# A second feed-forward pass moved from its own phase into the main steps

## The chip, the cores and the metric

The kernel runs on one core of a Trainium2 chip. TensorE multiplies, VectorE and ScalarE work on SBUF and PSUM, GpSimd works on SBUF, and SyncE issues most DMAs. The metric is the device time of one execution in microseconds; runs are compared by their median.

## The reference, cut to what matters

The input x is 32 images of 96 channels by 28 x 28 (784 tokens), float32. Three stages are each added to what they read:

```python
x = x + conv(_gn(x), ...)       # group norm, 4 experts of 96 -> 96 -> 96 by 1x1 convolutions, top 2 gated
t = tokens(x)
t = t + attn(_ln_t(t), ...)     # 12 heads of 8; fk = fv = where(t >= 0, t + 1, exp(t)); A = fk.v * gauss
t = t + ffn(_ln_t(t), W1, b1, W2, b2)
# ffn: y1 = x Wb1 + b1 (384 wide, weights are signs); h = gelu(quant(y1)); y2 = h Wb2 + b2; out = quant(y2)
# quant, per group of 6 images (5 groups; images 30 and 31 stay 0):
#   clip(a * 128 / (max|a| + 1e-5), -128 + 1e-5, 128 - 1e-5)
```

The quantisation needs the largest absolute value over six whole images before any of them can go on, once for y1 (384 channels) and once for y2 (96 channels).

## The kernel before, in words

A **setup** (to about 66 us) loads x, takes group-norm statistics, prepares weights and gates. Then there are two phases.

The **main phase** handles one image a step, as a software pipeline over three images: step i runs the experts of image i, the attention of image a = i - 1 and the first feed-forward pass of image f = i - 2. Steps 0 to 3 and 30 to 32 are written out, the others are a hardware loop over pairs. TensorE in a step: the expert hidden tiles (`hidden`, L994), transposes of the attended image to tokens (`to_tokens`, L862), x1 transposed to channels into slot 0, the expert mix (`mix`, L1010), keys and values in two parts (`kv`, L1055), transposes of tok2 into slot 2 and of t1cm into slot 1, the A matmuls (L1158), three up-projection tiles (`ffn_tile`, L1017 and L1020) with three small matmuls chained between them, and the output matmuls (L1187). PSUM is four slots of two banks; each slot has several users in a step, and each user waits for the reader before it.

ScalarE in a step (`step`, L748): three relus, copies from PSUM (tok2, xh1T, tok1, St, R), two exps (L759), the cast of the normalised tokens to `big`, and last `norm_image` (L725), which normalises image i + 2 and makes its f16 high part. VectorE (`step`, L1464): layer-norm statistics and apply (L1423, L1430, L1436), the residual t1cm, feature maps (L1470), the low part (L1514), the mask of A, the absolute maximum of each y1 tile straight from PSUM (`absmax`, L1440), t2T. GpSimd (`step`, L606): the low part of the next image (`xn_rest`, L578), and the inverse root of the variance for two layer norms (`rstd`, L598). Of the first feed-forward pass only the maxima of y1 are kept; the normalised tokens stay in `big` as two f16 parts, and SyncE stores t2 to `out` in HBM.

The **feed-forward phase** begins when all 30 maxima are there. For each image TensorE computes y1 once more (`ffn_up`, L1200), ScalarE applies gelu with the scale and casts the high part of two tiles (`gelu_tile`, `gelu_hi`, L813 and L819), VectorE makes the low parts and clips (`split`, L1550), TensorE projects down (`ffn_down`, L1210), ScalarE evacuates y2 (L829), VectorE takes its maximum, and after six images a scale; images of the group before are scaled, clipped and added to the stored t2, which SyncE loads back and stores (`clipped`, L1577). The last group of six follows alone.

All order is that of the five instruction streams as written; engines meet only at semaphores. A queue that waits holds all that is behind it.

## Time and profile before

| | us |
|---|---|
| median of 3 runs | 830.09 (829.99 to 832.92) |
| the profiled execution: span from first to last instruction | 829.6 |
| lowest timed run less that span (what lies around it) | 0.4 |
| PE busy, of the span | 769.0 (93%) |
| DVE busy | 636.5 (77%) |
| ACT busy | 476.7 (57%) |
| POOL busy | 180.2 (22%) |

The profiled execution has no time of its own beside its span in the profile, so the timed runs stand for it. Busy time is what an engine spent in instructions, averaged over stages with different limits; which wait ends last in a stage is read from that stage. PE is TensorE, DVE VectorE, ACT ScalarE, POOL GpSimd. L12 is line 12 of the kernel.

### The profile page before, as it was taken

Reading aid. Unit: us, or ns where it says so; the run is one execution under the profiler, and the core shown is the slowest. Engines: PE = TensorE matmul, PEld = TensorE weight load, DVE = VectorE, ACT = ScalarE, POOL = GpSimd, SP = SyncE. Lnnn points to the kernel's source line nnn. Section 1 sums busy time; section 2 is a strip of 40 time slices with the busy share of each in tenths; the row PEclk is TensorE's granted clock in tenths of the full one; section 3 lists DMA queues with packets and bytes.
Section 4 is the critical chain, followed back from the end, with each engine's and each line's share of the span. In section 5 each row is a group of like instructions: output and inputs, shape, how many; then the busy total and the mean of one; then the engine's idle time right before and its main releaser. Section 6 shows DMA issues by size and latency. Waiting matters only on the chain.

```text
span 829.6 us, 15136 instructions
## 1 busy us (share of the span) xinstructions
PE 769.0 (93%) x4663; PEld 510.4 (62%) x4663; DVE 636.5 (77%) x1945; ACT 476.7 (57%) x684; POOL 180.2 (22%) x209
## 2 busy tenths in 40 slices
PE   6798899999999999999999999999999999999991
PEld 3465566667666667666666766666766555555540
DVE  3576377877888878788877778887778468999997
ACT  2554445545555554545554555554553499988981
POOL 1440222332223232223232223233222000000000
PEclk8899989999999999999999999999999999999996
DMA  9950011101101101111110101010100101463333
GB/s 217 207 138 16 16 30 30 46 29 29 44 29 29 44 29 29 44 29 29 42 31 29 43 30 29 29 43 29 30 28 15 32 28 53 147 179 113 119 117 116
DMA packets 20351, 48.62 MB, mean 59 GB/s; under 512 B 4937, under 2 KB 5223, under 8 KB 20327
## 3 DMA queue, kind: packets, MB, share of 16 engines
q1 hardware_dynamic: 19928, 47.72, 21.0%
q10 hardware_dynamic: 399, 0.60, 0.3%
q8 instruction: 13, 0.21, 0.1%
q14 instruction: 11, 0.09, 0.0%
HBM read 29.51 MB, written 18.67 MB: 58 GB/s over the span
## 4 chain that ended last, share of the span: by engine, by line
PE 68%; DVE 11%; ACT 8%; issue 7%; SPq 3%; POOL 2%; DMA 1%; ACTq 0%; DVEq 0%; POOLq 0%
PE slot L1010 15%; PE slot L994 9%; PE slot L1017 7%; PE slot L1020 6%; PE slot L1158 6%; PE slot L1055 5%; PE slot L1187 5%; PE slot L1218 4%; PE slot L1222 4%; PE slot L862 4%; DVE stage L1470 4%; ACT stage L759 3%; SPq L442 3%; ACT hT L752 2%; PE slot L926 1%
## 5 line engine op out<-in xcount | busy, mean ns | idle before, releaser
L1436 DVE TENSOR_SCALAR tok<-tok,ln_mv,ln_rs 112x96 f32<-112x96 f32 x434 | 109.2, 322 | 58.2 <-POOL ln_rs L603 58.2
L1010 PE MATMUL slot<-hT,w2s 128*96 128x392 f32 x384 | 135.5, 503 | 3.0 <-ACT hT L752 2.3
L759 ACT ACTIVATE stage<-slot,minus_one 112x768 f32<-112x768 f32 x64 | 52.6, 822 | 125.6 <-PE slot L1055 123.3
L752 ACT ACTIVATE hT<-slot,b1c,w_unit 128x784 f32<-128x784 f32 x96 | 93.1, 1006 | 23.0 <-PE slot L994 23.0
L1010 PEld LDWEIGHTS slot<-hT,w2s 128*96 128x96 f32 x384 | 60.6, 164 | 64.1 <-issue 54.4
L603 POOL TENSOR_TENSOR ln_rs<-ln_ve,pow_half 112x7 f32<-112x7 f32 x62 | 91.8, 1481 | 4.8
L1017 PE MATMUL slot<-big,W1b 99*128 (+1 forms) x360 | 90.3, 332 | 2.1 <-ACT hT L816 0.6
L1020 PE MATMUL slot<-big,W1b 96*128 (+1 forms) x360 | 89.8, 330 | 0.0
L816 ACT ACTIVATE hT<-slot,s 128x784 f32<-128x784 f32 x90 | 80.3, 926 | 6.6 <-DVE stage L1554 6.3
L1442 DVE TENSOR_REDUCE ymax<-slot 128x784 f32 (+1 forms) x90 | 81.1, 956 | 0.1
L600 POOL TENSOR_TENSOR ln_ve<-ln_mv,ln_eps 112x7 f32<-112x7 f32 x62 | 12.5, 202 | 316.2 <-DVE ln_mv L1430 316.2
L1055 PEld LDWEIGHTS slot<-qkvw,xh1T 97*112 97x112 f32 x448 | 73.6, 177 | 10.5 <-issue 9.5
L1423 DVE BATCH_NORM_STATS2 ln_st<-tok 112x6 f32<-112x96 f32 x434 | 75.0, 243 | 4.7 <-ACT tok L746 2.6
L1055 PE MATMUL slot<-qkvw,xh1T 97*112 97x192 f32 x448 | 78.3, 326 | 0.1
L580 POOL TENSOR_TENSOR xn_lo<-xn,xn_hi 96x784 f16<-96x784 f32 x32 | 54.4, 1699 | 102.5 <-DVE tok L1436 102.5
L1470 DVE SCALAR_TENSOR_TENSOR stage<-stage,slot 112x768 f32<-112x768 f32 x64 | 51.8, 849 | 28.2 <-ACT stage L759 28.2
L1554 DVE SCALAR_TENSOR_TENSOR stage<-hT,stage 128x784 f16<-128x784 f32 x60 | 56.6, 968 | 14.5 <-ACT stage L825 14.5
L1158 PE MATMUL slot<-stage 112*96 112x96 f32 x448 | 46.8, 257 | 12.9 <-DVE stage L1470 12.9
L746 ACT COPY tok<-slot 112x672 f32<-112x672 f32 x62 | 44.5, 718 | 24.7 <-PE slot L862 24.7
L862 PE MATMUL slot<-con,tok 112*96 112x112 f32 x434 | 52.1, 260 | 2.2 <-DVE tok L1436 2.2
L1158 PEld LDWEIGHTS slot<-stage 112*96 112x96 f32 x448 | 41.5, 168 | 19.7 <-DVE stage L1470 19.7
L1218 PE MATMUL slot<-stage,W2b 128*96 128x392 f16 x240 | 46.6, 334 | 5.7 <-DVE stage L1554 2.0
(190 smaller groups left out, 1285.2 us busy)
## 6 DMA issues: line engine op xcount, KB each, us to landing
out<-t2T SPq DMA_DIRECT2D x56, 294.0 KB, 2.6
xs<-in_x SPq DMA_DIRECT2D x32, 294.0 KB, 2.8
big<-in_x SPq DMA_DIRECT2D x7, 1176.0 KB, 15.3
xs<-out SPq DMA_DIRECT2D x24, 294.0 KB, 3.3
...
```

The costliest lines, as they stand in the source:

```text
L603: nc.gpsimd.tensor_tensor(ln_rs[n][:, :], ln_ve[n][:, :], pow_half[0:TOK, 0:CHUNKS], ALU.pow).then_inc(ln_rstd[n], 1)
L752: nc.scalar.activation(hT[:, t, :].rearrange("p (a n) -> p a n", a=2), halves(t, P), ACT.Relu, scale=w1_unit[:, t:t + 1], bias=b1c[:, t:t ...
L816: nc.scalar.activation(gel[:, t, :].rearrange("p (a n) -> p a n", a=2), halves(t, P), ACT.Gelu, scale=s1[:, bass.ds(g, 1)]).then_inc(gelu_ ...
L862: return mm(o, i, ident[0:rows, 0:rows], start=start, stop=True, is_transpose=True, skip_group_check=True)
L1010: ins = mm(S[k][0:C, h, 0:HALF], w2s[:, v, t, :], hT[:, t, h * HALF:(h + 1) * HALF], start=t == 0, stop=t == TILES - 1, skip_group_check=True)
L1017: mm(S[k][:, h, 0:HALF], w, big[:, f, 0, h * HALF:(h + 1) * HALF], start=True, stop=False, skip_group_check=True)
L1020: ins = mm(S[k][:, h, 0:HALF], w[0:C, :], big[0:C, f, 1, h * HALF:(h + 1) * HALF], start=False, stop=True, skip_group_check=True)
L1055: ins = mm(chunks(k, n, 256, 2 * C)[:, j, :], xh1T[:, (j0 + j) * TOK:(j0 + j + 1) * TOK], qkvw[:, C:3 * C], start=True, stop=True, skip_gr ...
L1158: ins = mm(S[3][0:C, 0, 0:C], fkv[:, j, 0:C], fkv[:, j, C:2 * C], start=j == 0, stop=j == CHUNKS - 1)
L1436: ins = V.tensor_scalar(dst[:, j, :], src[:, j, :], ln_mv[n][:, j, 0:1], ln_rs[n][:, j:j + 1], ALU.subtract, ALU.mult)
L1442: V.tensor_reduce(ymax[:, bass.ds(3 * f + t, 1)], halves(k, P), AX.XY, ALU.max, apply_absolute_value=True).then_inc(ymax_done, 1)
L1470: V.scalar_tensor_tensor(fkv[:, j0:j0 + n, :], ekv[:, j0:j0 + n, :], 1.0, chunks(k, n, 256, 2 * C), ALU.min, ALU.max).then_inc(f_ready, 1)
```

## The change

There are now 40 written-out steps for every engine and no feed-forward phase. Step i also runs the gelu and split of image d = i - 9 and the down-projection of image e = i - 10, and finishes an image of the group before (i - 17 up to image 17, two a step in steps 35 to 37). The y1 tiles are kept in SBUF for eight images (ScalarE copies them out of PSUM, `keep_y1`), so the up-projection is done once; y2 is kept for eight images too. Maxima of y1 are taken from SBUF in the next step. Scales are made for one group at a time, in steps 8, 14, 20, 26, 32 for y1 and 16, 22, 28, 34 for y2, the last behind the steps. The cast of gelu's high part moves from ScalarE to GpSimd; scale, clip and add of most images move from VectorE to GpSimd in three operations. ScalarE normalises image i + 1 in the middle of step i instead of image i + 2 at its end. The transposes of t1cm go to slot 2 instead of slot 1, behind the reader of the tok2 transposes. The tiles share `over`, `big` and `stage` in another layout; the `two_ones` DMA is replaced by a memset. The last six images are finished by VectorE as before.

```diff
+Y1_RING, Y2_RING = 8, 8
+TO_GELU, TO_DOWN, TO_OUT = 9, 10, 17
+RB_IMAGES = 18
+STEPS = QIMAGES + TO_DOWN
+S1_STEP = {QB * g + QB + 2: g for g in range(QGROUPS)}
+S2_STEP = {QB * g + QB + TO_DOWN: g for g in range(QGROUPS)}
+OUT_STEP = {n + TO_OUT: [(n, "pool")] for n in range(RB_IMAGES)}
+OUT_STEP.update({35 + k: [(RB_IMAGES + 2 * k, "pool"), (RB_IMAGES + 2 * k + 1, "dve")] for k in range(3)})
+OUT_ORDER = [one for i in sorted(OUT_STEP) for one in OUT_STEP[i]]
+OUT_COUNT = {n: (by, sum(1 for m, b in OUT_ORDER if b == by and m <= n)) for n, by in OUT_ORDER}
...
+        x2 = sb("x2", [C + PARTS, 2, HW], F16)
+
+        def y1(b):
+            o = (Y2_RING + b % Y1_RING * TILES) * HW
+            return big[:, o:o + TILES * HW].rearrange("p (t n) -> p t n", n=HW)
+
+        def y2(b):
+            o = b % Y2_RING * HW
+            return big[0:C, o:o + HW]
...
+            def hi_part(d, t):
+                pool.wait_ge(gelu_ready, TILES * d + t + 1)
+                wait_count(pool, y2_ready, d - 1)
+                nc.gpsimd.tensor_copy(h_hi(d, t), y1(d)[:, t, :]).then_inc(hi_parts, 1)
+
+            outs = [0]
+
+            def finish(n):
+                pool.wait_ge(s2_ready, n // QB + 1)
+                nc.gpsimd.tensor_scalar(y2(n), y2(n), s2[:, n // QB:n // QB + 1], 1.0, ALU.mult,
+                                        ALU.mult).then_inc(y2_scaled, 1)
+                outs[0] += 1
+                pool.wait_ge(y2_scaled, outs[0])
+                nc.gpsimd.tensor_scalar(y2(n), y2(n), Q_CLIP, -Q_CLIP, ALU.min, ALU.max).then_inc(y2_clipped, 1)
+                pool.wait_ge(y2_clipped, outs[0])
+                residual_loaded(pool, n)
+                nc.gpsimd.tensor_tensor(residual(n), y2(n), residual(n), ALU.add).then_inc(out_by_pool, 1)
+
+            def step(i):
+                image, a, f, d, e = images(i)
+                if f is not None:
+                    rstd(1, f)
+                    pool.wait_ge(xh2_ready, f + 1)
+                if d is not None:
+                    for t in range(SPLIT):
+                        hi_part(d, t)
+                if image is not None and 2 <= i + 1 < BATCH:
+                    xn_rest(i + 1)
+                for n, by in OUT_STEP.get(i, ()):
+                    if by == "pool":
+                        finish(n)
+                if image is not None:
+                    rstd(0, i)
...
+            def normalise(i):
+                r = i % 2
+                if i >= FIRST:
+                    act.wait_ge(xs_loaded[r], 16 * (i // 2 + 1))
+                wait_count(act, z_ready, 3 * (i - 1))
+                wait_count(act, xn_lo_ready, i - 1)
+                nc.scalar.activation(xn[r][:, :], x_all[:, i, :] if i < FIRST else xs[r][:, :], ACT.Identity,
+                                     scale=gn_scale[:, i:i + 1], bias=gn_shift[:, i:i + 1]).then_inc(xn_made, 1)
+                act.wait_ge(xn_made, i - 1)
+                nc.scalar.copy(xn_hi[r][:, :], xn[r][:, :]).then_inc(xn_hi_made, 1)
+
+            def keep_y1(f, t):
+                act.wait_ge(y_ready, TILES * f + t + 1)
+                wait_count(act, y2_ready, f - Y1_RING + 1)
+                nc.scalar.copy(y1(f)[:, t, :].rearrange("p (a n) -> p a n", a=2), halves(t, P)).then_inc(y1_evac, 1)
+
+            def gelu(d):
+                g = d // QB
+                act.wait_ge(s1_ready, g + 1)
+                for t in range(TILES):
+                    nc.scalar.activation(y1(d)[:, t, :], y1(d)[:, t, :], ACT.Gelu,
+                                         scale=s1[:, g:g + 1]).then_inc(gelu_ready, 1)
+
+            def y2_out(e, k):
+                act.wait_ge(y2_ready, e + 1)
+                if e >= Y2_RING:
+                    out_done(act, e - Y2_RING)
+                nc.scalar.activation(y2(e).rearrange("p (a n) -> p a n", a=2), halves(k, C),
+                                     ACT.Identity, bias=fb2c[:, 0:1]).then_inc(y2_evac, 1)
...
+                    relu(1, 1)
+                if f is not None:
+                    act.wait_ge(tok2_in_psum, f + 1)
                     tokens(tok2, 3, tok2_ready)
-                if experts and not between:
-                    relu(1, 1)
+                if image is not None and i > 0:
                     relu(2, 2)
-                if attend:
-                    act.wait_ge(x1T_ready, i)
+                if a is not None:
+                    act.wait_ge(x1T_ready, a + 1)
                     nc.scalar.copy(*channels(xh1T[0:C, :], 0)).then_inc(xh1T_ready, 1)
+                if d is not None:
+                    gelu(d)
+                if a is not None:
                     exp_kv(0, 3, 0, CH_A)
-                if attend:
+                if f is not None:
+                    act.wait_ge(x2p_ready, f + 1)
+                    nc.scalar.copy(*channels(x2[0:C, 0, :], 2)).then_inc(hi_ready, 1)
+                if a is not None:
                     exp_kv(1, 0, CH_A, CHUNKS - CH_A)
-                if ffn:
-                    wait_apart(act, x2p_ready, i - 1, act_passed)
-                    nc.scalar.copy(*channels(big[0:C, i - 2, 0, :], 2)).then_inc(hi_ready, 1)
-                if experts:
+                if image is not None and 2 <= i + 1 < BATCH:
+                    normalise(i + 1)
+                if e is not None:
+                    y2_out(e, down_slot(e))
+                if image is not None:
                     act.wait_ge(tok1_in_psum, i + 1)
-                    tokens(tok1, 1, tok1_ready)
-                if between:
+                    tokens(tok1, 2, tok1_ready)
+                if i == 0:
                     act.wait_ge(signs_ready, 1)
                     nc.scalar.copy(W2last[:, :], W2b[:, TILES - 1, :])
                     gate_exps(1, 0)
-                if attend:
-                    act.wait_ge(stp_ready, i)
+                if a is not None:
+                    act.wait_ge(stp_ready, a + 1)
                     nc.scalar.copy(St[:, :], S[3][0:C, 1, 0:C + 1]).then_inc(st_ready, 1)
-                    act.wait_ge(rp_ready, i)
+                if f is not None:
+                    keep_y1(f, 0)
+                if a is not None:
+                    act.wait_ge(rp_ready, a + 1)
                     nc.scalar.copy(R[:, :], S[3][0:C + 1, 0, 0:C]).then_inc(r_ready, 1)
-                if experts and next_:
-                    norm_image(m + 1, r, i + 2)
-
-            step(0, 0, attend=False, ffn=False, between=True)
-            for i in range(1, FIRST):
-                step(i // 2, i % 2, ffn=i >= 2)
+                if f is not None:
+                    keep_y1(f, 1)
+                    keep_y1(f, 2)
...
+                if f is not None:
+                    pe.wait_ge(xh2_ready, f + 1)
+                    to_channels(2, tok2, x2p_ready)
+                if a is not None:
                     kv(1, 0, CH_A, CHUNKS - CH_A)
-                if scales:
-                    y1_max_row()
-                    keep_busy(1, 0, 9)
-                if ffn:
-                    pe.wait_ge(xh2_ready, i - 1)
-                    to_channels(2, tok2, x2p_ready)
-                if experts:
+                if e is not None:
+                    if image is not None:
+                        pe.wait_ge(t1_ready, i + 1)
+                    elif i == BATCH:
+                        pe.wait_ge(y1_evac, TILES * QIMAGES)
+                    else:
+                        pe.wait_ge(y2_evac, e - 1)
+                    down(e, down_slot(e))
+                if i in S1_STEP or i in S2_STEP:
+                    if a is not None:
+                        pe.wait_ge(f_ready, 2 * (a + 1))
+                    if i in S1_STEP:
+                        s1_row(S1_STEP[i])
+                    else:
+                        s2_row(S2_STEP[i])
+                if image is not None:
                     pe.wait_ge(t1_ready, i + 1)
-                    to_tokens(1, t1cm[r], tok1_in_psum)
+                    if f is not None:
+                        pe.wait_ge(lo_ready, f + 1)
+                    to_tokens(2, t1cm[r], tok1_in_psum)
...
+                if i in S1_STEP:
+                    s1_spread(S1_STEP[i])
+                elif i in S2_STEP:
+                    s2_spread(S2_STEP[i])
+                if f is not None:
+                    if i in S1_STEP:
+                        pe.wait_ge(s1e_ready, S1_STEP[i] + 1)
+                    elif i in S2_STEP:
+                        pe.wait_ge(s2e_ready, S2_STEP[i] + 1)
+                    pe.wait_ge(hi_ready, f + 1)
+                    pe.wait_ge(lo_ready, f + 1)
+                    ffn_tile(0)
...
+            def absmax(f, t):
+                dve.wait_ge(y1_evac, TILES * f + t + 1)
+                V.tensor_reduce(ymax[:, TILES * f + t:TILES * f + t + 1], y1(f)[:, t, :], AX.X, ALU.max,
                                 apply_absolute_value=True).then_inc(ymax_done, 1)
...
+            def split(d):
+                for t in range(SPLIT):
+                    dve.wait_ge(hi_parts, SPLIT * d + t + 1)
+                    V.scalar_tensor_tensor(h_lo(d, t), y1(d)[:, t, :], Q_CLIP, h_hi(d, t),
+                                           ALU.min, ALU.subtract).then_inc(parts_ready, 1)
+                dve.wait_ge(gelu_ready, TILES * (d + 1))
+                V.tensor_scalar(y1(d)[:, SPLIT, :], y1(d)[:, SPLIT, :], Q_CLIP, None, ALU.min).then_inc(parts_ready, 1)
+
+            clips = [0]
+
+            def finish(n, out, loaded, done):
+                g = n // QB
+                dve.wait_ge(s2_ready, g + 1)
+                V.tensor_scalar(y2(n), y2(n), s2[:, g:g + 1], Q_CLIP, ALU.mult, ALU.min).then_inc(tail_clip, 1)
+                clips[0] += 1
+                dve.wait_ge(tail_clip, clips[0])
+                loaded()
+                V.scalar_tensor_tensor(out, y2(n), -Q_CLIP, out, ALU.max, ALU.add).then_inc(done, 1)
...
+                if 3 <= i < QIMAGES + 3:
+                    absmax(i - 3, 0)
+                    absmax(i - 3, 1)
...
+                if 3 <= i < QIMAGES + 3:
+                    absmax(i - 3, 2)
+                if i > TO_DOWN:
+                    y2_absmax(i - TO_DOWN - 1)
+                if i in S1_STEP:
+                    s1_max(S1_STEP[i])
+                elif i in S2_STEP:
+                    s2_max(S2_STEP[i])
+                if a is not None:
                     feature_map(0, 3, 0, CH_A)
                     feature_map(1, 0, CH_A, CHUNKS - CH_A)
-                if ffn:
+                if f is not None:
                     dve.wait_ge(hi_ready, f + 1)
-                    V.tensor_tensor(tokenwise(big[0:C, f, 1, :]),
+                    V.tensor_tensor(tokenwise(x2[0:C, 1, :]),
                                     flat(2)[0:C, 0:CHUNKS * P].rearrange("p (j t) -> p j t", t=P)[:, :, 0:TOK],
-                                    tokenwise(big[0:C, f, 0, :]), ALU.subtract).then_inc(lo_ready, 1)
-                if attend:
-                    mask_a(i, 3)
-                if scales:
-                    y1_scale()
-                if experts:
+                                    tokenwise(x2[0:C, 0, :]), ALU.subtract).then_inc(lo_ready, 1)
+                if i in S1_STEP:
+                    s1_one(S1_STEP[i])
+                elif i in S2_STEP:
+                    s2_one(S2_STEP[i])
+                if d is not None:
+                    split(d)
+                if a is not None:
+                    dve.wait_ge(a_ready, a + 1)
+                    V.tensor_tensor(Am[:, :], S[3][0:C, 0, 0:C], gauss[:, :], ALU.mult).then_inc(am_ready, 1)
+                if i in S1_STEP:
+                    s1_scale(S1_STEP[i])
+                elif i in S2_STEP:
+                    s2_scale(S2_STEP[i])
+                if image is not None:
                     dve.wait_ge(tok1_ready, i + 1)
-                    stats(0, tok1, 1 if isinstance(i, int) and i == 0 else 2 * i)
-                if ffn:
-                    for t in range(TILES):
-                        absmax(f, t, t)
-                if attend:
-                    dve.wait_ge(ao_ready, i)
-                    wait_count(dve, t2T_stored[1 - r], 16 * (m + r - 1))
-                    V.tensor_tensor(t2T[1 - r][:, :].rearrange("p (a n) -> p a n", a=2), halves(3, C),
-                                    t1cm[1 - r][:, :].rearrange("p (a n) -> p a n", a=2),
+                    stats(0, tok1)
+                if a is not None:
+                    dve.wait_ge(ao_ready, a + 1)
+                    wait_count(dve, t2T_stored[a % 2], 16 * (a // 2))
+                    V.tensor_tensor(t2T[a % 2][:, :].rearrange("p (a n) -> p a n", a=2), halves(3, C),
+                                    t1cm[a % 2][:, :].rearrange("p (a n) -> p a n", a=2),
                                     ALU.add).then_inc(t2_ready, 1)
-                if experts:
+                if image is not None:
                     apply(0, tok1, tok1, i, xh1_ready)
-
-            for i in range(FIRST):
-                step(i // 2, i % 2, attend=i >= 1, ffn=i >= 2)
+                for n, by in OUT_STEP.get(i, ()):
+                    if by == "dve":
+                        finish(n, residual(n), lambda: residual_loaded(dve, n), out_by_dve)
```

## Rows read from the trace of the kernel before

**Rows 1.** Stages: stretch, length, busy us and count per engine, PEclk, DMA share, GB/s.

```profile
124.75:643.60 518.85, 504.59 (x3133) 354.91 (x3131) 412.26 (x1482) 276.27 (x375) 144.26 (x144) 1.00 0.11 33
393.19:411.14 17.95, 17.43 (x109) 12.24 (x108) 14.32 (x53) 9.55 (x14) 5.13 (x6) 1.00 0.12 34
...
658.70:814.30 155.60, 146.41 (x729) 81.37 (x727) 134.83 (x184) 143.20 (x181) 0.00 (x0) 1.00 0.36 105
814.30:829.60 15.30, 0.80 (x3) 0.47 (x3) 10.83 (x17) 0.00 (x0) 0.00 (x0) 0.53 0.46 138
```

**Rows 2.** TensorE, one step: start, us, line, operation, tiles, count, idle before.

```profile
396.82 0.85 PE L862 MATMUL slot<-con,tok 112*96 112x112 f32 x7
...
401.67 2.44 PE L1055 MATMUL slot<-qkvw,xh1T 97*112 97x192 f32 x14
...
405.78 1.43 PE L1158 MATMUL slot<-stage 112*96 112x96 f32 x14 [0.42 <-DVE stage L1470]
```

**Rows 3.** ScalarE in the same step.

```profile
398.37 0.81 ACT L777 COPY xh1T<-slot 96x784 f32<-96x784 f32 x1
403.17 1.72 ACT L759 ACTIVATE stage<-slot,minus_one 112x768 f32<-112x768 f32 x2 [4.00 <-PE slot L1055]
...
409.81 1.04 ACT L736 ACTIVATE xn<-xs,gn_shift,gn_scale 96x784 f32<-96x784 f32 x1 [0.21 <-issue]
410.96 0.84 ACT L739 CAST xn_hi<-xn 96x784 f16<-96x784 f32 x1
```

**Rows 4.** VectorE in the same step.

```profile
400.53 1.77 DVE L1436 TENSOR_SCALAR tok<-tok,ln_mv,ln_rs 112x96 f32<-112x96 f32 x7 [1.88 <-POOL ln_rs L603]
...
404.11 1.62 DVE L1470 SCALAR_TENSOR_TENSOR stage<-stage,slot 112x768 f32<-112x768 f32 x2 [0.87 <-ACT stage L759]
406.07 0.97 DVE L1514 TENSOR_TENSOR big<-slot,big 96x784 f32 x1 [0.34 <-ACT big L783]
```

**Rows 5.** GpSimd in the same step.

```profile
396.83 1.67 POOL L580 TENSOR_TENSOR xn_lo<-xn,xn_hi 96x784 f16<-96x784 f32 x1 [3.50 <-DVE tok L1436]
398.73 0.20 POOL L600 TENSOR_TENSOR ln_ve<-ln_mv,ln_eps 112x7 f32<-112x7 f32 x1 [0.23 <-DVE ln_mv L1430]
399.01 1.48 POOL L603 TENSOR_TENSOR ln_rs<-ln_ve,pow_half 112x7 f32<-112x7 f32 x1
```

**Rows 6.** GpSimd during the setup, three operations of 384 columns.

```profile
41.00 0.50 POOL L567 CAST part_h<-fb1r 3x384 bf16<-3x384 f32 x1
41.60 1.25 POOL L568 TENSOR_SCALAR part_c<-part_h,con 3x384 f32<-3x384 bf16 x1
42.94 0.99 POOL L569 TENSOR_TENSOR part_b<-fb1r,part_c 3x384 f32<-3x384 f32 x1
```

**Rows 7.** GpSimd and VectorE side by side, and the same VectorE operation alone.

```profile
105.21 2.49 POOL L580 TENSOR_TENSOR xn_lo<-xn,xn_hi 96x784 f16<-96x784 f32 x1 [2.24 <-DVE tok L1436]
...
65.35 0.21 DVE L1323 TENSOR_TENSOR stage<-stage 112x112 f32<-112x112 f32 x1
...
106.97 0.86 DVE L1323 TENSOR_TENSOR stage<-stage 112x112 f32<-112x112 f32 x1
```

**Rows 8.** ScalarE: the table load between the phases, and gelus later.

```profile
657.26 1.28 ACT L844 ACT_TABLE_LOAD   x1
658.56 0.20 ACT L844 ACTIVATE gelu_warm<-minus_one 112x1 f32<-112x1 f32 x1
...
800.86 1.72 ACT L816 ACTIVATE hT<-slot,s 128x784 f32<-128x784 f32 x2
```

**Rows 9.** Feed-forward phase: one down-projection on TensorE, one split on VectorE.

```profile
805.73 1.53 PE L1218 MATMUL slot<-stage,W2b 128*96 128x392 f16 x8
807.09 1.48 PE L1222 MATMUL slot<-stage,W2last 128*96 128x392 f32 x4
...
809.16 1.85 DVE L1554 SCALAR_TENSOR_TENSOR stage<-hT,stage 128x784 f16<-128x784 f32 x2
810.93 0.56 DVE L1557 TENSOR_SCALAR stage<-hT 128x784 f32<-128x784 f32 x1
```

641 lines of the change are left out of this document (239 added, 402 removed).

## The prediction

> **What bounds the kernel now.** I read the sum by stages first, then one main step on each engine, then the feed-forward phase. In the stage table TensorE is busy 504.59 of 518.85 us over the 29 steps from step 3 on; VectorE is busy 412, ScalarE 276, GpSimd 144 [rows 1]. The phase after it (30 images, 155.6 us) has ScalarE busy 143.20 us, so ScalarE bounds it there; the last group of six takes another 15.3 us with almost only VectorE at work [rows 1]. One main step lasts from 393.19 to 411.14, 17.95 us [rows 1], on TensorE back to back but for 0.42 us ahead of the A matmuls [rows 2]. The reader is to see in that step how much room the other engines leave: ScalarE sat idle 4.00 us ahead of its exp, because it had copied xh1T and kv came only after the expert mix [rows 3].
>
> From here X is the start of the transposes x1_to_channels in a step (396.82 in the row), since that is where the loops close.
>
> **What goes.** The recomputed up-projection (3 tiles an image), 24 of the store/reload/clip pipelines' VectorE pairs, and the phase of 155.6 us as a phase; of its parts, gelu, high part, low part, down-projection and evacuation come back inside the steps. The reduction of y1 moves from PSUM to SBUF behind three ScalarE copies an image.
>
> **Steps 0 to 8.** Nothing of the second pass runs yet. But the transposes of t1cm now go to slot 2 instead of slot 1, and wait for lo_ready, the subtraction that reads slot 2. The path: kv pass 0 needs the transposes and the mix, 401.67 - 396.82 = 4.85 us, and four sevenths of 2.44: it ends at X + 6.25 [rows 2]. Exp (0.9), the cast to x2 (I take the 0.81 us of the copy of the same size), second exp (0.9), feature map 0.85, subtraction 0.97 give X + 10.7 [rows 3, 4]; TensorE would be ready at X + 8.0. In the old order the A matmuls began at 405.78 - 396.82 = 8.96; now at 10.7 + 0.6 = 11.3. With 0.3 us more because R's copy stands behind the first evacuation of y1, a step is 20.6 us. This is 2.7 us on the path, not hidden by anything, in steps 2 to 8.
>
> **Steps 9 to 16.** Added on TensorE: the down-projection, 10 matmuls, 1.36 + 1.34 = 2.7 us at full clock [rows 9]; it lies exactly in the gap just described, so it costs nearly nothing. Added on ScalarE: three gelus (two take 1.72 us, a third 0.81: 2.55), three evacuations (2.7), y2_out (0.9). Gelu and Exp stand next to each other in each step. The load ahead of the first gelu took 1.28 us [rows 8], in a program whose exps run before it, so I count a load ahead of gelu and one ahead of exp: 2 x 1.3. ScalarE then works 9.55 [rows 1] + 2.7 + 2.55 + 0.9 + 2.6 = 18.3 us in a step: it fits, but not everywhere. xh1T is copied by X + 1.8 (the third relu stands ahead of it), then 1.3 + 2.55 + 1.3: exp starts at X + 7.0 and not 6.25. That puts lo at X + 11.3 and A at X + 11.9. The split of h (1.85 + 0.56 us on VectorE [rows 9]) stands between lo and the mask of A, until 13.75, and the rest of the step (two chained small matmuls, three up tiles, the output matmuls) ends at X + 17.8; the 3.6 us of the next step's head (393.19 to 396.82) follow, so: 21.3 us a step. The down-projection alone would be a floor of 17.95 + 2.7 = 20.7.
>
> The Trainium skill, "ScalarE: Activation LUTs", section "What ACT_TABLE_LOAD costs", gives 1.28 us plus a drain of 1.38 us for every change of set, 2.66 in all; the trace has the 1.28 and the next activation 0.02 us behind it, so it does not show the drain. By the page the sum would be 24 steps x 2.8 = 66 us longer.
>
> **Steps 17 to 31.** Now GpSimd's finish of an image (scale, clip, add) stands between xn_rest and rstd(0, i) in its queue, and rstd(0, i) is what the next step's apply waits for. No row shows a 96x784 TENSOR_SCALAR on GpSimd. From below: the 384-column cast took 0.50 us, so 784 columns would be 1.0. From above: the 384-column TENSOR_SCALAR took 1.25 us, so at most 2.55; with the 0.2 us that a 7-column operation takes there, the slope is 1.05 / 384 = 2.74 ns and the sum 0.2 + 784 x 2.74 ns = 2.35 [rows 5, 6]. I take 2.35 twice, because that row is the same operation with the same kind of pointer scalar. The add is a TENSOR_TENSOR: 0.99 us for 384, so 1.83. With waits 0.15, F = 6.7 us (bounds 4.0 and 7.1).
>
> The loop through it: xn_rest 1.7; F; rstd 0.2 + 0.08 + 1.48 = 1.8; apply 1.77; transposes 0.85; xh1T 0.81; load 1.3; gelus 2.55; load 1.3; exp, cast, exp 2.5; xn and its cast, 411.80 - 409.81 = 2.0; eight handovers at 0.04 = 0.3. That is 16.9 + F = 23.6 us a step [rows 3 to 5, 8], over TensorE's 21.3. So in 15 steps GpSimd sets the time, though it is busy for only about 14 us of each. It decides from F = 4.4 on.
>
> **Contention.** The SBUF side of GpSimd and VectorE is not free. One xn_lo took 2.49 us instead of 1.67 while VectorE ran two-input operations on SBUF, and one of those, of 112x112, took 0.86 us where it takes 0.21 [rows 7]. The split (two SBUF inputs, 1.85 us) will now meet xn_rest and finish in each step. Between 0 and 1.9 us a step on the loop, so 0 to 28 us; I take 0 for the sum, since either engine can be the one that waits and VectorE's split has slack in a 23.6 us step, and keep 28 for the range.
>
> **Scale steps.** In steps 8, 14 and 16 the two small reductions and the wait for s1e or s2e ahead of the first up tile cost about 1 us each (four small VectorE operations of 0.15 to 0.25 and three handovers); in 20, 22, 26, 28 they lie under GpSimd's loop.
>
> **The end.** From X of step 32: GpSimd casts h of image 23 (5.8), finishes image 15 (12.5); gelu of image 24 waits for its scale, its casts end at 17.4. Then each of five steps has two casts (0.95 each, estimated from the 0.50 for 384) and one finish: 8.6 x 5 gives 60.4; split, down, y2_out 5 us. Behind the last y2_out the tail is the old one, 15.3 us [rows 1, 9]. Together 80.7 us.
>
> **Sum.** X of step 3 is 128.4 now; with 2.1 more from step 2, 130.5. Then 6 x 20.6 = 123.6; 8 x 21.3 = 170.4; 3 for scale steps; 15 x 23.6 = 354; 80.7: 862.2 us, against a span of 829.6. The median of the runs is 0.5 us over that span, so 863 us. Less than 0.5% (4 us) is about what a measurement of this kernel cannot tell from no change.
>
> **Rivals.**
> 1. *The clip is cheap* (other side: faster). If a GpSimd TENSOR_SCALAR goes at the rate of its cast, F = 4.0, GpSimd drops out of the loop and TensorE's path through lo and A bounds all steps from 9: 427.5 + 15 x 21.3 + 4 (scale steps) + end 67 = 818 us. For it: the cast row [rows 6]. Against it: the TENSOR_SCALAR row beside it, 2.5 times as long. The time is about 728.2 + 20 F above F = 4.4, so the kernel gets slower than before from F = 5.1 on. The Trainium skill's "GPSIMD Engine Reference", section 4.1, calls one-input operations there "roughly line-rate"; that would be this case, and the row speaks against it.
> 2. *No table changes*: one set serves gelu and exp, contrary to how I read the load at 657.26. The loop loses 2.6 us: 21.0 in steps 17 to 31, 20.7 before: 254 + 166 + 3 + 315 + 80 = 818 us. For it: the row shows only that the first set lacked gelu, not that the second lacks exp.
> 3. *Loads or contention cost more*: the split's 1.9 us falls on GpSimd's loop each time, 862 + 28 = 891 us; with both drains of the page it would be over 900. For it: rows 7. Against: the idle time in the loop for VectorE.
> 4. *TensorE packs better than I count*, with the lo wait mostly hidden in all steps and the clip cheap: 128.4 + 7 x 18 + 22 x 20.7 + 67 = 777 us is the floor that TensorE's work sets.
>
> **How the numbers follow.** The forecast (GpSimd's loop, 845 to 885) 0.48; rival 1 0.22; rival 2 0.08; rival 3 0.12; rival 4 0.05; mixtures near the old time 0.05. Faster by over 0.5%: 0.22 + 0.08 + 0.05 and a little of the mixtures, 0.36; same 0.06; slower 0.58. The range takes the forecast, rivals 1 and 2 and the lower part of rival 3: 803 to 888. The forecast's own range is 845 to 885.
>
> **What would show it.** Right: GpSimd TENSOR_SCALAR of 96x784 at 2.2 to 2.5 us; steps 17 to 31 at 23 to 25 us with TensorE's transposes of tok waiting for VectorE's tok, and that for GpSimd's ln_rs; two ACT_TABLE_LOADs in each of steps 9 to 32; TensorE transposes of t1cm waiting for VectorE's x2 in steps 2 to 8, by 2 to 3 us. Wrong: TENSOR_SCALAR near 1 us, or steps 17 to 31 no longer than steps 10 to 16, or no loads in the steps; then the time falls to 818 or below. The step lengths of 2 to 8 and 9 to 16 test the rest by themselves.

## The result and the profile after

The changed kernel takes 838.28 us (median of 4 runs, 836.62 to 839.36) against 830.62 us for the kernel before on the same chip: ratio 1.0083, interval 1.006 to 1.0106. It is slower, as forecast, but by 7.7 us and not by 33. Its span is 836.7 us (before 829.6), its mean granted TensorE clock 0.941 (before 0.975). TensorE's work fell from 769.0 to 719.5 us; GpSimd's rose from 180.2 to 345.4.

Stages after, in the columns of [rows 1], each from one ScalarE copy of R to another: from step 2's to step 8's, to step 16's, to step 31's, and the rest. R is copied once in each step, so the distance of two copies is a step's length.

```profile
118.60:250.20 131.60, 116.07 (x652) 83.93 (x651) 86.78 (x314) 70.46 (x98) 31.46 (x31) 0.88 0.10 29
250.20:423.80 173.60, 157.97 (x956) 109.81 (x955) 146.28 (x446) 140.03 (x175) 59.06 (x55) 0.99 0.11 31
423.80:751.90 328.10, 300.73 (x1814) 205.17 (x1813) 276.53 (x840) 262.97 (x329) 175.18 (x149) 1.00 0.19 54
751.90:836.70 84.80, 46.89 (x158) 26.98 (x156) 59.48 (x79) 33.43 (x40) 45.73 (x34) 0.72 0.42 114
```

A plain step was 17.95 us. It is now 21.1 to 23.0 us in steps 3 to 8 and 21.8 in most of steps 9 to 31. In the scale steps 20, 22, 26 and 28 it is 21.2 up to the copy of R and then 23.0 to the next one. Before, the span ended 172.6 us behind step 32's copy of R (657.0); now it ends 65.0 us behind it, but that copy comes at 771.7. So 107.6 us are saved at the end, and 114.7 us are paid up to it.

ScalarE in one step after [rows 3, 8], from the first load to the first exp behind the second. The load ahead of the gelus and the load ahead of the exps are both there, 1.28 us each, and the next activation follows at once.

```profile
518.90 1.28 ACT L806 ACT_TABLE_LOAD   x1
520.19 2.63 ACT L806 ACTIVATE big<-big,s 128x784 f32<-128x784 f32 x3
522.84 1.28 ACT L828 ACT_TABLE_LOAD   x1
524.13 0.90 ACT L828 ACTIVATE stage<-slot,minus_one 112x768 f32<-112x768 f32 x1
```

GpSimd in two steps after [rows 5, 6]: the low part, then the three operations of finish, then rstd(0, i).

```profile
505.90 3.75 POOL L617 TENSOR_TENSOR xn_lo<-xn,xn_hi 96x784 f16<-96x784 f32 x1 [3.84 <-ACT xn_hi L795]
509.75 0.91 POOL L652 TENSOR_SCALAR big<-big,s 96x784 f32<-96x784 f32 x1
510.76 0.84 POOL L656 TENSOR_SCALAR big<-big 96x784 f32<-96x784 f32 x1
511.68 1.84 POOL L659 TENSOR_TENSOR over<-big,over 96x784 f32<-96x784 f32 x1
...
513.75 1.49 POOL L640 TENSOR_TENSOR ln_rs<-ln_ve,pow_half 112x7 f32<-112x7 f32 x1
...
528.25 2.22 POOL L617 TENSOR_TENSOR xn_lo<-xn,xn_hi 96x784 f16<-96x784 f32 x1 [4.14 <-ACT xn_hi L795]
530.56 1.91 POOL L652 TENSOR_SCALAR big<-big,s 96x784 f32<-96x784 f32 x1
```

VectorE in the same two steps [rows 4, 7, 9]: the split, and the apply behind rstd(0, i).

```profile
505.81 1.84 DVE L1483 SCALAR_TENSOR_TENSOR stage<-big,stage 128x784 f16<-128x784 f32 x2
...
515.28 1.76 DVE L1436 TENSOR_SCALAR tok<-tok,ln_mv,ln_rs 112x96 f32<-112x96 f32 x7 [1.86 <-POOL ln_rs L640]
...
527.95 3.34 DVE L1483 SCALAR_TENSOR_TENSOR stage<-big,stage 128x784 f16<-128x784 f32 x2
...
537.09 1.77 DVE L1436 TENSOR_SCALAR tok<-tok,ln_mv,ln_rs 112x96 f32<-112x96 f32 x7 [0.69 <-POOL ln_rs L640]
```

Read the last two fences together. The first pair is a scale step, the second a plain one. GpSimd's TENSOR_SCALAR over 784 columns takes 0.84 to 0.91 us alone, not 2.35. But it is not always alone. At 505.81 VectorE's split starts first; xn_lo, issued 0.09 us later, lasts 3.75 us, about the 1.84 of the split more than its own 1.67 [rows 5] and 0.2 beside. At 527.95 the first half of the split starts, xn_lo at 528.25 ends at 530.47, the second half of the split ends only at 531.29, and GpSimd's scale, issued at 530.56, takes 1.91 instead of 0.91 since it ends after that. The operations take turns, and who goes first decides which chain gets longer: the low part loses 2.1 us in the first pair, the split 1.5 us in the second. The Trainium skill, "SBUF — State Buffer", section "SBUF: two separate sides", calls VectorE's and GpSimd's common port pair an "exclusive lock", "not a bandwidth split", which whoever starts first holds for a whole instruction. The second pair agrees, and [rows 7] had shown that there are such waits; in the first pair the low part waits for two instructions, not one.

The groups of all such instructions after (line, count, busy us, mean ns, idle before):

```profile
L617 POOL TENSOR_TENSOR xn_lo<-xn,xn_hi 96x784 f16<-96x784 f32 x32 | 74.6, 2331 | 143.2 <-ACT xn_hi L795 143.2
...
L652 POOL TENSOR_SCALAR big<-big,s 96x784 f32<-96x784 f32 x21 | 37.0, 1760 | 2.1
L806 ACT ACT_TABLE_LOAD x25 | 32.1, 1283 | 0.5
```

These means run over the whole program. In steps 17 to 31 alone a plain step has 2.22 us for the low part and 1.91 for the scale, a scale step 3.75 and 0.91.

The chain of waits through steps 9 to 16, without GpSimd (start, us, piece): it returns to the copy of xh1T after 21.81 us; behind it come the two loads with the gelus, the exps, the subtraction, then the rows shown, and from the mask on TensorE's small and output matmuls, the next hidden tile and the relus.

```profile
300.78 0.69 ACT xh1T L846
...
310.62 3.26 DVE stage L1483 x2
313.88 0.48 DVE big L1486
314.36 0.18 DVE Am L1570
...
322.59 0.70 ACT xh1T L846
```

### The profile page after: what moved, and what is told of

The parts are those of the page before. It is cut to its first block, busy times and chain, and to the rows that moved or that the text cites. A ratio compares the mean times of both kernels' runs of the same rounds, so it can differ in the third digit from the quotient of the medians.

```text
span 836.7 us, 12386 instructions
## 1 busy us (share of the span) xinstructions
PE 719.5 (86%) x4290; PEld 487.8 (58%) x4290; DVE 639.4 (76%) x1918; ACT 558.9 (67%) x761; POOL 345.4 (41%) x332
## 3 DMA queue, kind: packets, MB, share of 16 engines
q1 hardware_dynamic: 19928, 47.72, 21.6%
## 4 chain that ended last, share of the span: by engine, by line
ACT 31%; PE 31%; DVE 21%; POOL 7%; issue 5%; SPq 3%; DMA 2%; POOLq 0%; DVEq 0%
ACT hT L821 7%; DVE stage L1483 7%; ACT big L806 7%; ACT stage L828 5%; PE slot L1024 5%; PE slot L1249 4%; ACT L806 4%; ACT L828 3%; PE slot L1040 3%; PE slot L892 3%; PE slot L1047 3%; PE slot L1050 3%; DVE x L1559 3%; DVE stage L1508 3%; PE slot L1215 2%
## 5 line engine op out<-in xcount | busy, mean ns | idle before, releaser
L617 POOL TENSOR_TENSOR xn_lo<-xn,xn_hi 96x784 f16<-96x784 f32 x32 | 74.6, 2331 | 143.2 <-ACT xn_hi L795 143.2
L1040 PE MATMUL slot<-hT,w2s 128*96 128x392 f32 x384 | 131.8, 493 | 0.4 <-ACT hT L821 0.4
L1105 PE MATMUL slot<-qkvw,xh1T 97*112 97x192 f32 x448 | 86.5, 335 | 0.9 <-ACT xh1T L846 0.9
L1483 DVE SCALAR_TENSOR_TENSOR stage<-big,stage 128x784 f16<-128x784 f32 x60 | 82.3, 1410 | 4.2 <-POOL stage L646 4.2
L1442 DVE TENSOR_REDUCE ymax<-big 128x1 f32<-128x784 f32 x90 | 82.9, 950 | 0.0
L1581 DVE TENSOR_TENSOR t2T<-slot,t1cm 96x784 f32<-96x784 f32 x32 | 31.1, 971 | 67.7 <-PE slot L1249 67.7
L806 ACT ACTIVATE big<-big,s 128x784 f32<-128x784 f32 x90 | 78.8, 938 | 0.3
L646 POOL CAST stage<-big 128x784 f16<-128x784 f32 x60 | 50.9, 873 | 57.7 <-DVE tok L1436 43.0
L800 ACT COPY big<-slot 128x784 f32<-128x784 f32 x90 | 70.3, 818 | 0.1
L1508 DVE SCALAR_TENSOR_TENSOR stage<-stage,slot 112x768 f32<-112x768 f32 x64 | 53.9, 848 | 16.7 <-ACT stage L828 14.5
L869 ACT COPY St<-slot 96x97 f32<-96x97 f32 x32 | 7.6, 237 | 82.3 <-PE slot L1232 82.3
L892 PE MATMUL slot<-con,t1cm 96*112 96x96 f32 x224 | 27.0, 267 | 35.1 <-DVE x L1559 34.0
```

The lines of the kernel that those rows point to most:

```text
L806: nc.scalar.activation(y1(d)[:, t, :], y1(d)[:, t, :], ACT.Gelu, scale=s1[:, g:g + 1]).then_inc(gelu_ready, 1)
L892: return mm(o, i, ident[0:rows, 0:rows], start=start, stop=True, is_transpose=True, skip_group_check=True)
L1040: ins = mm(S[k][0:C, h, 0:HALF], w2s[:, v, t, :], hT[:, t, h * HALF:(h + 1) * HALF], start=t == 0, stop=t == TILES - 1, skip_group_check=True)
L1105: ins = mm(chunks(k, n, 256, 2 * C)[:, j, :], xh1T[:, (j0 + j) * TOK:(j0 + j + 1) * TOK], qkvw[:, C:3 * C], start=True, stop=True, skip_gr ...
L1442: V.tensor_reduce(ymax[:, TILES * f + t:TILES * f + t + 1], y1(f)[:, t, :], AX.X, ALU.max, apply_absolute_value=True).then_inc(ymax_done, 1)
L1483: V.scalar_tensor_tensor(h_lo(d, t), y1(d)[:, t, :], Q_CLIP, h_hi(d, t), ALU.min, ALU.subtract).then_inc(parts_ready, 1)
```

## The experiments

Times are medians; each ratio is to the kernel before on the same chip, with its 95% interval. The kernel before has 830.3 to 831.2 us on each of these chips, so times of different runs can be compared too. Unless said, the edit is to the kernel after. Step lengths are taken from one copy of R to the next.

**Are the table loads the price?** `e1_no_tables`:

```diff
-                    nc.scalar.activation(y1(d)[:, t, :], y1(d)[:, t, :], ACT.Gelu,
+                    nc.scalar.activation(y1(d)[:, t, :], y1(d)[:, t, :], ACT.Relu,
```

> The gelu is replaced by a relu with the same scale, so this kernel leaves the gelu out of the computation and needs no second table set. Theory A (in steps 9 to 31 the chain is ScalarE: load, three gelus, load, exps, then VectorE's split, then the mask of A): both loads are on it, 2.6 us in each of 23 steps, but TensorE's own work is a floor of 20.7 us a step where 21.8 is measured, so 1.0 to 1.2 us a step or 23 to 28 us come back: 810 to 815 us. Theory B (GpSimd's queue through finish sets steps 17 to 31): its loop also runs through both loads, so it gives the same there; the two part in steps 9 to 16 only. Theory C (contention and the split alone set it, the loads lie in idle time): 836 to 840 us.

848.52 us, 1.0213 (1.0165 to 1.026): slower than with the loads. A miss for every theory. Steps 9 to 16 do shorten, to 20.2 in plain steps. Steps 17 to 31 alternate between about 20.2 and 24.6 to 27.8. The stages of one such pair, in the columns of [rows 1], the chain of waits in the long one, and VectorE's split beside its low part:

```profile
528.20:555.60 27.40, 22.92 (x124) 15.38 (x123) 19.91 (x62) 15.12 (x21) 16.06 (x15) 0.89 0.15 45
555.60:576.30 20.70, 20.10 (x122) 13.94 (x121) 16.99 (x54) 15.24 (x21) 8.50 (x7) 0.98 0.20 59
```

```profile
523.74 4.23 POOL xn_lo L617
...
532.08 1.50 POOL ln_rs L640
...
533.60 1.78 DVE tok L1436 x7
...
536.55 5.45 PE slot L1040 x12
...
547.97 3.04 DVE stage L1483 x2
```

```profile
524.11 1.85 DVE L1483 SCALAR_TENSOR_TENSOR stage<-big,stage 128x784 f16<-128x784 f32 x2
```

With the gelus earlier, the low part meets both halves of the split (4.23 us for 1.67, while the split keeps its 1.85). TensorE waits 1.84 us for the apply that stands behind ln_rs, and then the granted clock falls: the mix takes 5.45 us, where it takes 4.12 in the short step behind, and the clock of the long step is 0.89 on average. So a wait on GpSimd's loop seems to be paid again on TensorE. This compares two kernels with other timing throughout; that the waits cause the lower clock is read from their order, not isolated.

**Is finish in front of rstd(0, i) the price?** `e2_rstd_first`:

```diff
+                if image is not None:
+                    rstd(0, i)
                 for n, by in OUT_STEP.get(i, ()):
                     if by == "pool":
                         finish(n)
-                if image is not None:
-                    rstd(0, i)
```

> GpSimd does rstd(0, i) ahead of the finish of an image, instead of behind it. Theory B (GpSimd's queue sets steps 17 to 31): the loop loses 3.8 us, the step falls until ScalarE and the split bound it: if these alone would give 21.2, 10 us less, 828 us. Theory A (ScalarE's chain and the split): no change, 836 to 840 us, or a little slower, since finish now overlaps VectorE's apply and lengthens it.

853.5 us, 1.0261 (1.0211 to 1.031). Also a miss: plain steps 18 to 31 go from 21.8 to 23.1. Finish leaves the wait but lands beside the apply, on which the next step's transposes wait (1.3 us in each of these steps). VectorE and GpSimd in one step:

```profile
541.92 3.33 DVE L1436 TENSOR_SCALAR tok<-tok,ln_mv,ln_rs 112x96 f32<-112x96 f32 x5
```

```profile
543.27 1.92 POOL L659 TENSOR_TENSOR over<-big,over 96x784 f32<-96x784 f32 x1
```

Five of the seven parts of the apply take 3.33 us; all seven take 1.76 elsewhere.

**Is it the split's place?** `e3_split_late` puts VectorE's split behind the mask of A and the statistics of tok1:

```diff
-                if d is not None:
-                    split(d)
                 if a is not None:
                     dve.wait_ge(a_ready, a + 1)
...
                     stats(0, tok1)
+                if d is not None:
+                    split(d)
```

> VectorE splits h behind the mask of A and the statistics of tok1 instead of ahead of them. Theory A with the split on the path: from lo on, A and its mask no longer wait for 3.7 us of split; A itself ends 2.7 us behind lo, so about 1 us a step or 20 us come back, 816 to 820 us, if t2T and apply, which now wait for the split, do not take it back. Theory B (GpSimd's loop): in steps 17 to 31 nothing changes, or it gets worse because the split meets finish; only steps 9 to 16 gain, 8 us: 830 us.

822.89 us, 0.9906 (0.9876 to 0.9936). Plain steps 9 to 16 become 20.4, steps 17 to 31 about 21.6. The low part is alone again (32 of them; columns: count, busy us, mean ns, idle before):

```profile
L617 POOL TENSOR_TENSOR xn_lo<-xn,xn_hi 96x784 f16<-96x784 f32 x32 | 53.6, 1676 | 144.5 <-ACT xn_hi L795 144.5
```

After, that row has a mean of 2331 ns. So the split was on the chain in steps 9 to 16, as forecast: with it moved, a plain step is 1.4 us shorter. In steps 17 to 31 the gain is 0.2 us a plain step. There the late split meets GpSimd's finish instead and takes 3.43 us, and TensorE waits 1 us for the t2T that stands behind it. Theory A held in steps 9 to 16 and theory B in steps 17 to 31.

**Is slot 2 the price in steps 2 to 8?** `e4_slot1_early` puts the transposes of t1cm back in slot 1 in steps 0 to 9, with the waits that this needs:

```diff
+        def tok1_slot(i):
+            return 1 if i < TO_DOWN else 2
...
-                    tokens(tok1, 2, tok1_ready)
+                    tokens(tok1, tok1_slot(i), tok1_ready)
...
+                    pe.wait_ge(tok1_ready, i)
...
-                    if f is not None:
+                    if f is not None and tok1_slot(i) == 2:
                         pe.wait_ge(lo_ready, f + 1)
-                    to_tokens(2, t1cm[r], tok1_in_psum)
+                    to_tokens(tok1_slot(i), t1cm[r], tok1_in_psum)
...
+                    if tok1_slot(i) == 1:
+                        pe.wait_ge(tok1_ready, i + 1)
```

> In steps 0 to 9 the transposes of t1cm go to slot 1, as before the change, and do not wait for the low part. If the slot is the reason why steps 2 to 8 take 22.4 us instead of 18.5, they fall by 3 us each: 21 us, and step 9 by about 1: 815 to 819 us. If it is ScalarE's copies of y1 (2.4 us more a step), nothing or little: 834 to 840 us.

814.26 us, 0.9793 (0.9748 to 0.9838): 24 us less than after, from a few steps. (The profiled execution, of 823.7 us, was the longest of five and 15 us shorter than after's: its steps 8 to 10 were still 22.7 to 23.5 us. In e5 below, with the same slot, they are 19.4 to 20.5.) TensorE in step 4 after, where it waits [rows 2], then the stretch of the lower clock, and last the stage of steps 3 to 7 of e4 without the wait:

```profile
155.42 1.34 PE L892 MATMUL slot<-con,t1cm 96*112 96x96 f32 x7 [2.59 <-DVE x L1559]
156.55 2.45 PE L1215 MATMUL slot<-stage 112*96 112x96 f32 x14
```

```profile
154.90:161.70 6.80, 6.28 (x32) 5.22 (x33) 2.32 (x16) 2.17 (x4) 2.19 (x3) 0.50 0.00 0
```

```profile
138.30:210.40 72.10, 67.94 (x435) 48.85 (x433) 57.82 (x211) 46.40 (x64) 20.14 (x20) 1.00 0.12 35
```

The wait is 2.59 us (forecast 2.7), and the A matmuls behind it take 2.45 us, 1.43 before [rows 2]. TensorE is idle from 152.8 to 155.4, and from 154.9 to 161.7 the granted clock is 0.50, the lower of its two levels (1.2 GHz instead of 2.4); over that step of 22.6 us it is 0.85 on average. In e4 the same steps are 18.0 us at a clock of 1.00.

**Both together**, `e5_split_late_slot1` (the edits of e3 and e4):

> Both edits that gained by themselves: the split behind the statistics of tok1 (15 us less than the changed kernel), and slot 1 for the transposes of t1cm in steps 0 to 9 (24 us less). They act in different steps, so they should add: 838 - 15 - 24 = 799 us, perhaps 802 because steps 9 to 16 meet both. If they share a cause, 808 or more.

797.0 us, 0.9597 (0.9565 to 0.9629). The gains add, as expected: they lie in different steps for the most part.

**Is GpSimd's share of the end the price?** `e6_end_on_vector` lets VectorE finish images 18, 20 and 22 too:

```diff
-OUT_STEP.update({35 + k: [(RB_IMAGES + 2 * k, "pool"), (RB_IMAGES + 2 * k + 1, "dve")] for k in range(3)})
+OUT_STEP.update({35 + k: [(RB_IMAGES + 2 * k, "dve"), (RB_IMAGES + 2 * k + 1, "dve")] for k in range(3)})
```

> Only the images 18, 20 and 22, in steps 35 to 37, are finished by VectorE instead of GpSimd. If contention is what stretches VectorE's finish there (1.12 and 2.49 us instead of 0.62 and 0.97 us), a step falls from 7.9 us to 3.4 + 2 x 1.6 + waits = 6.9 us, and the end by 3 us: 835 us. If VectorE's work alone is the bound, it gets longer by 3 x 1.6 = 5 us: 843 us.

837.65 us, 1.0079 (1.0055 to 1.0104), the same as after. The traces show where the gain went. VectorE's finish is indeed at 0.62 + 0.97 us in most of these steps, but there are two of them, and the split is still stretched by GpSimd's casts (3.14 us in one step): a step is 7.5 us instead of 7.95. The end behind step 32's copy of R is 62.9 us instead of 65.0. But the first hidden tile of step 0 started at 64.0 instead of 62.7 in that execution, so a gain of 2 us at the end is about as large as what the start varies by.

**Is the finish on GpSimd the price?** `e7_all_on_vector` gives all of them to VectorE (`{n + TO_OUT: [(n, "dve")] ...}` beside the edit of e6):

> All finishes go to VectorE (0.62 + 0.97 us an image at the end of a step); GpSimd clips nothing. Contention theory: in steps 17 to 31 the split and xn_lo still collide, but GpSimd's queue is 3.7 us shorter, and a step is 21.8 us or less as in steps 9 to 16, minus nothing: 833 to 838 us. Theory that VectorE has no room: 1.6 us more in each of 15 steps, 855 to 860 us.

823.77 us, 0.9908 (0.9885 to 0.9932), 14.5 us less than after and better than either theory. Steps 18 to 31 are 20.6 (21.5 in scale steps), steps 9 to 16 stay at 21.8. So steps with a finish on VectorE are shorter than steps with no finish at all. The low part on GpSimd and the split on VectorE in one of them:

```profile
570.90 3.81 POOL L617 TENSOR_TENSOR xn_lo<-xn,xn_hi 96x784 f16<-96x784 f32 x1 [3.38 <-ACT xn_hi L795]
```

```profile
570.86 1.85 DVE L1483 SCALAR_TENSOR_TENSOR stage<-big,stage 128x784 f16<-128x784 f32 x2
```

In plain steps 9 to 17 of the same run the low part starts 0.3 us behind the split and takes 2.2 us, and the split 3.3. In steps 18 to 30 it starts 0.04 us behind it (0.2 to 0.3 ahead in scale steps), and the split keeps its 1.85 us. The low part's 3.8 us cost nothing there, since GpSimd has no finish behind it. So two things changed at once, the finish's place and who of the two waits; no run separates them.

`e8_late_slot1_vector` is e5 and e7 together:

> Split late, slot 1 early, and all finishes on VectorE. Contention theory: steps 17 to 31 fall from 21.6 (late split with GpSimd's finish) to about 20.6 to 20.9, as steps 9 to 16 of the late-split kernel (20.4) plus some of the 1.6 us: 785 to 792 us. Theory that VectorE has no room (18.3 + 1.6 us of work in a step of 20.7): 800 to 805 us.

789.96 us, 0.9512 (0.9482 to 0.9542), as the first theory has it. Steps 3 to 7 are 18.0, 9 to 17 mostly 20.4, 18 to 31 20.7 to 21.9. The finish's 14.5 us of e7 are only 7.0 us on top of e5: the late split and the finish on VectorE remove in part the same waits.

`e9_vector_no_tables` is e7 with e1's edit, so the loads go while GpSimd has no finish:

> Relu in place of gelu (so the gelu is left out) and all finishes on VectorE. Taking the loads away alone made the kernel 10 us slower; in steps 9 to 16 it gained 1.6 us a step, in 17 to 31 it lost up to 6 us in every second step. If that loss came from GpSimd's finish meeting VectorE's split (and the slower TensorE clock behind the waits), it is gone here: 20.2 to 20.4 us in all steps from 9 to 31, that is 20 us less than with the finishes on VectorE and the loads in place: 802 to 806 us. If it came from the shorter ScalarE chain itself, 825 us or more.

819.17 us, 0.9854 (0.983 to 0.9878). Expected was a gain of some 20 us over e7; it is about 5. Taking out 2.6 us of ScalarE a step brings steps 17 to 31 nothing (20.6 both times), because another chain stands at that length. ScalarE is not on it: it runs through TensorE's second half of a step and VectorE, with the finish (L1493, L1497) in it, and returns after 20.6 us:

```profile
563.31 0.76 PE slot L892 x7
...
567.77 1.33 PE slot L1249 x4
...
570.02 1.75 DVE tok L1436 x7
571.77 0.55 DVE big L1493
572.34 0.97 DVE over L1497
...
575.42 1.48 POOL ln_rs L640
577.17 1.53 DVE tok L1436 x6
...
583.94 0.76 PE slot L892 x7
```

**Does GpSimd's loop set steps 17 to 31?** From both sides. `e10_clip_twice`:

```diff
-                pool.wait_ge(y2_clipped, outs[0])
+                pool.wait_ge(y2_clipped, 2 * outs[0] - 1)
+                nc.gpsimd.tensor_scalar(y2(n), y2(n), Q_CLIP, -Q_CLIP, ALU.min, ALU.max).then_inc(y2_clipped, 1)
+                pool.wait_ge(y2_clipped, 2 * outs[0])
```

> The changed kernel with GpSimd's clip done twice (the second one changes nothing): F grows by 0.85 + 0.1 us. Theory that GpSimd's queue sets steps 17 to 31 (and 32 to 34): each such step grows by 0.95 us, 15 + 3 steps: 853 to 856 us. Theory that ScalarE's chain and the split set them: 838 to 842 us.

857.99 us, 1.0334 (1.0297 to 1.0371): 19.7 us for one more clip of 0.84 us a step. Steps of 21.8 become 22.8, and in each of steps 18 to 31 TensorE's transposes wait for VectorE's tok (1.0 us in plain steps); after, they do so in four steps only. Three of the long scale steps have a clock of 0.93 and 24.7 to 25.0 us. `e12_clip_left_out` takes the clip out instead:

```diff
-                nc.gpsimd.tensor_scalar(y2(n), y2(n), Q_CLIP, -Q_CLIP, ALU.min, ALU.max).then_inc(y2_clipped, 1)
-                pool.wait_ge(y2_clipped, outs[0])
```

> The kernel after the change, with GpSimd's clip of the finish left out (the largest reduced value then passes unclipped: part of the computation is left out), so 0.95 us less per step on GpSimd, by the same operation that the clip done twice doubled. If GpSimd's loop alone sets steps 17 to 31, 15 to 18 steps give 0.95 us each back and the time is 820 to 824 us. If it ties at 21.8 us per step with the chain of ScalarE's loads and gelus and VectorE's split, as steps 9 to 16 suggest, those steps stay at 21.4 to 21.8 us and the time is 834 to 838 us; then the added operation counted and the removed one does not.

831.12 us, 0.9997 (0.9981 to 1.0012), between the two ranges and 3 us from the second. The plain steps stay at 21.8; the four scale steps of 23.0 become 22.0, and some 3 us come in the end. In e12's steps the apply waits for nothing (compare 537.09 after):

```profile
536.70 1.75 DVE L1434 TENSOR_SCALAR tok<-tok,ln_mv,ln_rs 112x96 f32<-112x96 f32 x7
```

Adding 0.9 us costs it in nearly every step, removing it gives it back in four: GpSimd's loop (22.75 - 0.94 = 21.8 us by e10) and the chain through the loads, gelus and split (21.8 us in steps 9 to 16, where there is no finish) are of one length in plain steps.

**The best of these with a cheaper end.** In the last steps after, VectorE and GpSimd both finish images and stretch one another. VectorE's scale and add, then GpSimd's add of another image (1.84 us alone):

```profile
793.24 1.19 DVE L1493 TENSOR_SCALAR big<-big,s 96x784 f32<-96x784 f32 x1
794.47 2.48 DVE L1497 SCALAR_TENSOR_TENSOR xs<-big,xs 96x784 f32<-96x784 f32 x1
```

```profile
794.10 2.02 POOL L659 TENSOR_TENSOR xs<-big,xs 96x784 f32<-96x784 f32 x1
```

`e11_e8_high_part_scalar` is e8, with the cast of gelu's high part back on ScalarE from step 33 on, so that GpSimd has nothing there:

```diff
-                if d is not None:
+                if d is not None and i <= BATCH:
                     for t in range(SPLIT):
                         hi_part(d, t)
...
+                    if d + TO_GELU > BATCH and t > 0:
...
+                        nc.scalar.copy(h_hi(d, t - 1), y1(d)[:, t - 1, :]).then_inc(hi_parts, 1)
```

> The fastest version so far (split late, slot 1 early, finishes on VectorE; 790 us) with the high part of gelu cast by ScalarE from step 33 on, where it has no other work, so that GpSimd is idle there. If contention still stretches VectorE's split there (3.06 and 2.4 us instead of 1.85), it gives back 1 us in each of 5 or 6 steps: 784 to 786 us. If the end is bound by VectorE's sum alone, 789 to 791 us.

784.52 us, 0.9445 (0.9422 to 0.9469), the fastest of all and 53.8 us below the change as made. VectorE's split in the last steps, in e8 and then here:

```profile
749.87 3.14 DVE L1489 SCALAR_TENSOR_TENSOR stage<-big,stage 128x784 f16<-128x784 f32 x2
```

```profile
748.32 1.85 DVE L1494 SCALAR_TENSOR_TENSOR stage<-big,stage 128x784 f16<-128x784 f32 x2
```

All of VectorE's operations are at their own length here. A step is 6.2 us instead of 7.5, and the end behind step 32's copy of R is 56.4 us instead of 63.1 in e8 and 65.0 after.

## Why the prediction was right in sign and wrong in size

By the prediction's own terms, each from an X to the next X of the trace after (123.95, 255.74, 429.18, 756.66; scale steps put where they fall):

| term | forecast | measured |
|---|---|---|
| X of step 3 | 130.5 | 123.95 |
| six steps to X of step 9 | 124.6 | 131.8 |
| eight steps to X of step 17 | 172.4 | 173.4 |
| fifteen steps to X of step 32 | 354 | 327.5 |
| to the end of the span | 80.7 | 80.0 |
| sum | 862.2 | 836.7 |

- **The failed step is F**, GpSimd's finish of an image, 6.7 us in the forecast: 2.35 us for each TENSOR_SCALAR, scaled from a 384-column row of 1.25 us [rows 6] over the cast row beside it. That row reads bf16 on 3 partitions; the float32 form on 96 partitions takes 0.91 with a pointer scalar (the scale) and 0.84 with constants (the clip). The add was right (1.83 forecast, 1.84). Alone, F is about 3.8 us, below even the lower bound of 4.0. The fifteen steps that F was to set came out 26.5 us shorter than forecast. Rival 1 had this price. Which property made the 384-column row slow was not tried.
- **The sign was luck in part.** With F at 3.8 us the prediction's own working gives rival 1's 818 us, faster than before. The kernel is slower because of terms that the forecast put at nothing or too low, contention first.
- **Both of the prediction's signs of being wrong came**: TENSOR_SCALAR near 1 us, and steps 17 to 31 no longer than steps 10 to 16 (21.8 us in plain steps of both). The time of 818 or less that was to follow did not. Against rival 1's sum 18.7 us are missing: 1.7 up to X of step 17, 4.0 in the fifteen steps (323.5 with their scale steps, measured 327.5), and 13.0 at the end (67 and 80.0).
- **Contention was counted as 0.** In the last steps it is the largest part: VectorE's split, clip, scale and add take 2.4 + 1.2 + 1.2 + 2.5 us in each of steps 35 to 37 where 1.85 + 0.56 + 0.62 + 0.97 are their own lengths, 3.3 us more a step, and with GpSimd idle there and all finishes on VectorE (e11) the end is 8.6 us shorter. In a plain step from 17 on, the low part and the scale together take 1.55 us more than alone, so F with contention is 5.3 us and not 3.8. e10 puts that loop at 21.8, so the rest of it is 16.5 us (16.9 forecast). That is the length of the other chain, which has no finish in it. The bound of 1.9 us a step held for plain steps; in scale steps the low part alone takes 2.1 us more. The equal length is why one more clip costs in full (e10) and one less pays only in the scale steps and at the end (e12).
- **Steps 9 to 16** came out at 173.4 for 172.4, by the path forecast (loads, gelus, subtraction, split, mask of A). Inside it the split took 3.26 and not 1.85, and e3 shows what that place costs: 1.4 us a plain step. Other terms must have been somewhat too long to compensate; which was not separated. The floor of 20.7 that the prediction set for TensorE's work was too high: e3's steps are 20.4 with TensorE busy for 19.6, and e1's shortest are 20.2. (A down-projection is 12 matmuls [rows 9], not 10; its 2.7 us hold.)
- **Steps 3 to 8** were 7.2 us too short in the forecast. The wait was right (2.59 for 2.7), but after it TensorE ran slower: a mean clock of 0.85 to 0.92 in such steps. The forecast priced a wait on TensorE at its own length; here its matmuls behind it were longer too. e4 removes both, and with them the low clock.
- **The start** is 6.5 us earlier than forecast. The first hidden tile of step 0 is at 62.74 instead of 66.54. In the twelve other profiled kernels with the same setup it lies between 62.2 and 65.6, so part of that is how one execution differs from another. Step 1 is 3.4 us shorter up to its X: its mix waits 0.35 us instead of 2.25 and takes 4.16 instead of 5.66, since the normalisation no longer stands ahead of its relus. The prediction priced neither the memset in place of the DMA nor the normalisation's new place. No run separates them.
- **The end** agrees, by luck, with errors that cancel: a smaller finish, but VectorE's and GpSimd's operations stretched (above), and step 32 with TensorE at its lower level (kv, 2.44 us in [rows 2]):

```profile
756.66 1.51 PE L892 MATMUL slot<-con,tok 112*96 112x112 f32 x7 [2.83 <-DVE tok L1436]
759.07 4.82 PE L1105 MATMUL slot<-qkvw,xh1T 97*112 97x192 f32 x14 [0.90 <-ACT xh1T L846]
```

- **Table loads**: two in each step, 1.28 us each, with nothing between them and the activations around them but 0.01 to 0.02 us, as read. Rival 2 fell. But they were not worth the 2.6 us a step that its sum gave: without them a plain step from 9 to 16 is 1.6 us shorter, and in steps 17 to 31 other chains hold (e9) or it gets worse (e1).
- **Rival 3** named the right thing (the split on GpSimd's loop) on top of a wrong F. **Rival 4**'s 20.7 a step is passed in steps 9 to 16 of e3, e5 and e8 (20.4, with the split out of the way) and in e1, so it was no floor.

So where did the removed phase go? It came back as 3.9 us more in most main steps, on chains over four engines, and TensorE's busy time fell by 49.5 us only. Three of the prices were avoidable, each taken by itself: slot 2 early (24 us), the split's place (15 us), and finishes on GpSimd beside VectorE (14.5 us). Together they are 48.3 us (e8), since the last two overlap.
